# A Mamba and mixture-of-experts block on one core: the first state of batches 1 to 5 is multiplied by C's column in the banks

## The reference, cut to what matters

```python
delta = softplus(dt_raw @ dt_proj_w.T + dt_proj_b)          # 512 x 256 per batch
dA  = exp(einsum('bti,is->btis', delta, A))                 # 16 states s
dBu = einsum('bti,bts->btis', delta * u, B_ssm)
def step(h, inp):
    dA_t, dBu_t, C_t = inp
    h = dA_t * h + dBu_t
    return h, einsum('bis,bs->bi', h, C_t)
y = ys + u * D_param
y = y * silu(z)                                             # z gate
out = y @ out_proj_w.T + residual
# experts: h = silu(xf @ w_gate[e]) * (xf @ w_up[e]); out += gate * (h @ w_down[e])
```

## Time and profile before

| | |
|---|---|
| median of 3 runs | 611.23 us (609.09 to 611.37) |
| the profiled execution | 612.7 us, its span 610.9 us |
| PE, PEld | 541.7 us (89%), 422.0 us (69%) |
| DVE | 586.8 us (96%) |
| ACT, POOL | 459.0 us (75%), 490.1 us (80%) |
| mean granted clock of PE | 0.972 |

### The profile page before, as it was taken

The page is one execution under the profiler, slowest core; times in us unless marked ns, Lnnn a source line. Parts: engine busy times, 40 slices in busy tenths (PEclk is TensorE's granted clock), DMA queues, the critical chain, the costliest instruction groups (busy, mean ns, idle before and its releaser), DMA issues.

```text
span 610.9 us, 11399 instructions
## 1 busy us (share of the span) xinstructions
PE 541.7 (89%) x3558; PEld 422.0 (69%) x3558; DVE 586.8 (96%) x851; ACT 459.0 (75%) x927; POOL 490.1 (80%) x383
## 2 busy tenths in 40 slices
PE   5999889898898998999989999899989797768887
PEld 2377666656787778877887777877777565647564
DVE  6799989999999999999999999999999998998997
ACT  3699697259857888579876798667984589968880
POOL 2792466569999799988999889998997967875684
PEclk9899898979999999999999999999999899998999
DMA  7330219724796887879868898687874455323364
GB/s 194 111 130 1 74 32 251 280 81 160 253 314 217 282 283 236 305 236 310 294 171 309 283 291 298 209 288 248 282 261 155 155 222 193 104 99 104 80 134 90
DMA packets 61038, 122.48 MB, mean 200 GB/s; under 512 B 8362, under 2 KB 41778, under 8 KB 53938
## 3 DMA queue, kind: packets, MB, share of 16 engines
q1 hardware_dynamic: 53826, 112.42, 53.8%
q0 software_dynamic: 6144, 9.00, 7.1%
q10 hardware_dynamic: 1008, 0.33, 0.3%
HBM read 112.25 MB, written 9.47 MB: 199 GB/s over the span
## 4 chain that ended last, share of the span: by engine, by line
PE 53%; ACT 18%; DVE 15%; issue 12%; POOL 1%; ACTq 1%; DVEq 0%; POOLq 0%
PE bank L1483 9%; PE bank L1449 9%; PE bank L1601 8%; DVE bank L1161 6%; PE bank L1615 6%; PE bank L1609 5%; DVE h_sb L1178 5%; ACT dbu L556 3%; ACT bank L540 3%; ACT da L528 2%; PE bank L1506 2%; PE bank L1412 2%; PE bank L1498 2%; PE bank L1582 1%; PE bank L1357 1%
## 5 line engine op out<-in xcount | busy, mean ns | idle before, releaser
L948 POOL TENSOR_TENSOR dbu<-du,xn_all 128x1024 f32<-128x1024 f32 x86 | 203.7, 2369 | 24.4 <-DVE bank L1161 20.8
L1161 DVE TENSOR_TENSOR_SCAN bank<-bank,dbu 128x512 f32<-128x512 f32 x170 | 207.3, 1222 | 0.8
L1178 DVE TENSOR_TENSOR h_sb<-bank,xh_all 128x512 f32<-128x512 f32 x240 | 159.4, 678 | 1.2
L540 ACT ACTIVATE bank<-delta,a_sb 128x512 f32<-128x512 f32 x170 | 116.7, 688 | 38.2 <-DVE h_sb L1178 35.6
L1449 PE MATMUL bank<-id_sb,h_sb 128*128 128x128 f32 x992 | 132.7, 278 | 10.9 <-DVE h_sb L1178 9.4
L1449 PEld LDWEIGHTS bank<-id_sb,h_sb 128*128 128x128 f32 x992 | 113.5, 143 | 21.5 <-DVE h_sb L1178 14.7
L1161 DVE TENSOR_TENSOR_SCAN bank<-da,bank 128x512 f32<-128x512 f32 x82 | 96.3, 1213 | 6.2 <-PE bank L1412 5.1
L1601 PEld LDWEIGHTS bank<-wd_sb,hid 117*128 117x128 f32 (+1 forms) x432 | 54.7, 190 | 49.5 <-DVE hid L1212 29.3
L1601 PE MATMUL bank<-wd_sb,hid 117*128 117x128 f32 (+1 forms) x432 | 64.1, 284 | 18.7 <-ACT xT L721 16.5
L932 POOL DMA_INDIRECT xs<-xn_rows,src x72 | 70.4, 978 | 12.5 <-issue 9.0
L556 ACT ACTIVATE dbu<-du_t,bc_sb 128x256 f32<-128x256 f32 x164 | 69.4, 497 | 6.3 <-PE bank L1412 3.3
(11 more groups left out here) (200 smaller groups left out, 887.9 us busy)
## 6 DMA issues: line engine op xcount, KB each, us to landing
xh_all<-b_rows SPq DMA_DIRECT2D x30, 1024.0 KB
xn_all<-b_rows SPq DMA_DIRECT2D x25, 1024.0 KB
wgu_sb<-in_w_gu SPq DMA_DIRECT2D x72, 352.0 KB
wd_sb<-in_w_dn SPq DMA_DIRECT2D x72, 192.0 KB
y_slots<-ys SPq DMA_DIRECT2D x72, 64.0 KB
xn_rows<-xn_all SPq DMA_DIRECT2D x2, 1040.0 KB, 10.2
out<-x_sb SPq DMA_DIRECT2D x7, 256.0 KB
x_sb<-in_x SPq DMA_DIRECT2D x2, 640.0 KB, 6.0
```

The costliest lines, as they stand in the source:

```text
L540: nc.scalar.activation(bank_of(b, m)[:, :], delta[b % 2][:, hf, :], ACT.Exp, scale=a_sb[:, hf, k:k + 1]).then_inc(s["da_rdy"], 1)
L948: nc.gpsimd.tensor_tensor(dbu[k % 2][:, :, :], du[b % 2][:, :, :], b_ring[c % 2][:, k % CH, :].unsqueeze(1).to_broadcast([P, NH, T]), ALU. ...
L1161: nc.vector.tensor_tensor_scan(at, da_of(n)[:, hf, :] if n in IN_SBUF else at, inp, 0.0, ALU.mult, ALU.add).then_inc(s["h_rdy"], 1)
L1178: nc.vector.tensor_tensor(h_sb[k % 2][:, hf, :], bank_of(b, 2 * k + hf)[:, :], row, ALU.mult).then_inc(s["p_rdy"], 1)
```

## The change

In batches 1 to 5 (`BY_SCALAR`, steps 16, 32, 48, 64, 80) the scan of step 0 writes its state to `h_sb`, and there is no product for it. PE's `accumulate` of that step stands at the end of step 0, and not behind `up` in step 1. In step 1 ACT multiplies the four 128x256 pieces in banks 2 and 3 in place by C's column (`multiplied`); the sum of step 1 waits for that (`hc_rdy`). The column comes from `own_columns`: four PE transposes of 32 rows and a copy of 128x4 by ACT, for batch 1 in step 7 of batch 0, for batch 2 in step 5 of batch 1, for batches 3 to 5 in step 3 of the batch before. PE's `y_turn` stands ahead of `gate` in step 0. ACT's +1 of the z gate stands behind the next decay, `rounded` at the front of step 5 (end of step 4 before), `corrected` at the front of step 7 (end of step 5 before), the copy of `rows` and the multiplications ahead of `ys`. Waits on `p_rdy` count without the products that are gone (`by_vector`); where a bank's last reader was such a product the wait is for the scan (`bank_read`).

```diff
--- before.py
+++ after.py
@@ -197,7 +197,7 @@
                    first1 first2 first3 first4 first5 first6 first7 both0 both1 both2 both3 both4 both5 both6 both7 part_mm comb dbuT_a sp_corr a_ready stats_bn st rms_rt xn_w xh_w
                    xh_pe xhT_c lgmm oh_out rt top_rdy sel_rdy tot_mm tot_out rk_out slot_rdy texp_rdy lohi_rdy lo_rdy hi_set hi_rdy map_mm src_rdy
                    exp_rt x_pad acc_w g_mm u_mm bct_rdy dbu_p row_mm dbu_0 b_st b_in0 b_in1 c_in0 c_in1
-                   br_mm dbu_rdy da_rdy h_rdy p_rdy acc_mm y_out dd_rdy xc_mm x_th x_half u_rdy v_mm
+                   br_mm dbu_rdy da_rdy h_rdy p_rdy hc_rdy cc_mm cc_rdy acc_mm y_out dd_rdy xc_mm x_th x_half u_rdy v_mm
                    v_out bc_mm bc_rdy z_mm z_rdy z_one o_ev sp_exp sp_ln sp_rem sp_w sp_sum z_th delta_rdy du_rdy
                    dut_mm dut_rdy yb_mm g_rdy o_mm o_rdy o_out""".split()
         s = {k: sem(k) for k in names}
@@ -237,6 +237,19 @@
         def pooled_before(n):
 
             return sum(m < n for m in BY_POOL)
+
+        BY_SCALAR = [S * b for b in range(1, NB - 2)]
+
+        def by_vector(m):
+
+            return m - sum(min(max(m - 2 * n, 0), 2) for n in BY_SCALAR)
+
+        def bank_read(eng, m):
+
+            if m > 0 and (m - 1) // 2 in BY_SCALAR:
+                wait(eng, "h_rdy", m)
+            else:
+                wait(eng, "p_rdy", by_vector(m))
 
         def da_of(n):
 
@@ -257,6 +270,7 @@
         assert n0 == 2 * NT
 
         SKIPPED = {6: (1, 2), 7: (2, 4)}
+        COLUMN_TILE = {TILE[(b - 1) * S + (7 if b == 2 else 5)]: b for b in range(2, 6)}
         ROWS_AT = {b: 1 if b == 6 else 0 for b in range(NB - 1)}
         STEPS_AT = {b: (4, 6) if b == 6 else (2, 3) for b in range(NB - 1)}
         LOG_AT = {b: 10 if b == 6 else 9 for b in range(NB - 1)}
@@ -352,7 +366,7 @@
 
             def out_rows_in(b, c):
 
-                wait(sp, "p_rdy", 2 * S * b + 2 * CH * (c - 1) if b else 0)
+                wait(sp, "p_rdy", by_vector(2 * S * b + 2 * CH * (c - 1)) if b else 0)
                 spread_rows(c_ring[c % 2], b * 2 * S + S + c * CH, CH).then_inc(s[f"c_in{c % 2}"], 16)
 
             def own_rows(i):
@@ -532,7 +546,7 @@
 
                 b, k = n // S, n % S
                 m = 2 * k + hf
-                wait(act, "p_rdy", freed(b, m))
+                bank_read(act, freed(b, m))
                 if b == 6 and m == 2:
                     act.wait_ge(s["dut_rdy"], 3)
                 if k == 0:
@@ -592,6 +606,7 @@
                     vanishing(1, k - 7)
                 if k == 8:
                     totals_out()
+                    own_columns(1)
                 if k == 9:
                     spread_choices()
                     rounded(1)
@@ -630,6 +645,9 @@
                         scaled(g + 1)
                 if b < 6 and k == LOG_AT[b]:
                     logarithm(b + 1)
+                if g - 1 in BY_SCALAR:
+                    rows(b + 1)
+                    multiplied(g - 1)
                 if prev is not None and not (b < 6 and k == LOG_AT[b]):
                     out_out(prev)
                 if more:
@@ -640,6 +658,8 @@
                     scaled(g + 2)
                 if b < 6:
                     decay_bank(g + 1, 0)
+                    if k in z_step(b):
+                        z_plus(b, k)
                     if k == LOG_AT[b] and prev is not None:
                         out_out(prev)
                 elif b == 6 and k + 1 < S and g + 1 not in BY_PE:
@@ -660,8 +680,12 @@
 
             def early(b, k):
 
-                if k == ROWS_AT[b] + 1:
+                if b == 6 and k == ROWS_AT[b] + 1:
                     rows(b + 1)
+                if b < 6 and k == 5:
+                    rounded(b + 1)
+                if b < 6 and k == 7:
+                    corrected(b + 1)
                 if k in STEPS_AT[b]:
                     magnitudes(b + 1, STEPS_AT[b].index(k))
                 if b < 6 and k == PROJECT_AT[b] + 1:
@@ -675,9 +699,8 @@
 
                 if k in STEPS_AT[b]:
                     vanishing(b + 1, STEPS_AT[b].index(k))
-                if k == STEPS_AT[b][1] + 1:
+                if b == 6 and k == 7:
                     rounded(b + 1)
-                if k == (7 if b == 6 else 5):
                     corrected(b + 1)
                 if k == COLS_AT.get(b):
                     columns(b + 1)
@@ -696,15 +719,38 @@
                         act.wait_ge(s["dbuT_a"], S - 1)
                     nc.scalar.activation(du_t[:, hf, :], z_bank(b)[:, :], ACT.Copy)
                 nc.scalar.activation(zs_sb[:, hf, :], z_bank(b)[:, :], ACT.Tanh, scale=0.5).then_inc(s["z_th"], 1)
-                if 0 < b < 6:
-                    act.wait_ge(s["z_th"], 2 * b + i + 1)
-                    nc.scalar.activation(zs_sb[:, hf, :], zs_sb[:, hf, :], ACT.Identity, bias=sign_sb[:, 0:1]).then_inc(s["z_one"], 1)
+
+            def z_plus(b, k):
+
+                i, hf = z_turn(b, k), z_step(b)[k]
+                act.wait_ge(s["z_th"], 2 * b + i + 1)
+                nc.scalar.activation(zs_sb[:, hf, :], zs_sb[:, hf, :], ACT.Identity, bias=sign_sb[:, 0:1]).then_inc(s["z_one"], 1)
 
             def projected(b):
 
                 act.wait_ge(s["o_mm"], b + 1)
                 act.wait_ge(s["z_rdy"], 2 * b + 3)
                 nc.scalar.activation(du_t[:, 1, :], FB[0][:, :], ACT.Copy).then_inc(s["o_ev"], 1)
+
+            def multiplied(n):
+
+                b, k = n // S, n % S
+                i0 = BY_SCALAR.index(n)
+                if 0 < b < 6:
+                    act.wait_ge(s["cc_rdy"], b)
+                for i in range(2):
+                    act.wait_ge(s["acc_mm"], 2 * n + i + 1)
+                    for t in (2 * i, 2 * i + 1):
+                        last = nc.scalar.activation(HT[i][:, t % 2, :], HT[i][:, t % 2, :], ACT.Copy,
+                                                    scale=bc_sb[b % 2][:, t, S + k:S + k + 1])
+                    last.then_inc(s["hc_rdy"], 1)
+
+            def own_columns(c):
+
+                act.wait_ge(s["cc_mm"], c)
+                at = XHB if c == 1 else XD
+                nc.scalar.activation(bc_sb[c % 2][:, :, S:S + 1], at[:, 2 * P:3 * P].rearrange("p (t c) -> p t c", t=TT)[:, :, S:S + 1],
+                                     ACT.Copy).then_inc(s["cc_rdy"], 1)
 
             def y_evac(b):
 
@@ -717,6 +763,8 @@
             def slots_out(j):
 
                 act.wait_ge(s["xt_mm"], j + 1)
+                if j in COLUMN_TILE:
+                    own_columns(COLUMN_TILE[j])
                 wait(act, "u_mm", j - 1)
                 nc.scalar.activation(xT[j % 2][:, :], XD[:, 0:P], ACT.Copy).then_inc(s["xt_rdy"], 1)
                 if j == 0:
@@ -1008,7 +1056,7 @@
                     if i == 0:
                         pool.wait_ge(s["h_rdy"], 2 * (S * b + k) + 1)
                     else:
-                        pool.wait_ge(s["p_rdy"], 2 * (S * b + k) + i)
+                        pool.wait_ge(s["p_rdy"], by_vector(2 * (S * b + k) + i))
                     gathered(b0, c, t)
 
             scaled(S)
@@ -1157,19 +1205,25 @@
                 if b == NB - 1 and k == 1 and hf == 0:
                     dve.wait_ge(s["dut_rdy"], 6)
                 elif b == NB - 1 and k == 1:
-                    wait(dve, "p_rdy", 2 * S * b + 1)
-                nc.vector.tensor_tensor_scan(at, da_of(n)[:, hf, :] if n in IN_SBUF else at, inp, 0.0,
+                    bank_read(dve, 2 * S * b + 1)
+                to = at
+                if n in BY_SCALAR:
+                    to = h_sb[k % 2][:, hf, :]
+                    wait(dve, "acc_mm", 2 * (n - 1))
+                nc.vector.tensor_tensor_scan(to, da_of(n)[:, hf, :] if n in IN_SBUF else at, inp, 0.0,
                                              ALU.mult, ALU.add).then_inc(s["h_rdy"], 1)
 
             def product(b, k, hf):
 
                 c = k // CH
+                if b * S + k in BY_SCALAR:
+                    return
                 if b == 0 and c < 2:
                     if k % 2 == 0 and hf == 0:
                         dve.wait_ge(s[f"c_own{k // 2}"], 16)
                     row = own[k // 2][:, k % 2, :]
                 else:
-                    if k % CH == 0 and hf == 0:
+                    if hf == 0 and (k % CH == 0 or b * S + k - 1 in BY_SCALAR):
                         dve.wait_ge(s[f"c_in{c % 2}"], 16 * ((b - 1) * 2 + c // 2 + 2) if b else 16)
                     row = c_ring[c % 2][:, k % CH, :]
                 if hf == 0:
@@ -1394,6 +1448,8 @@
 
                 pe.wait_ge(s["lo_rdy"], g + 1)
                 pe.wait_ge(s["hi_rdy"], g + 1)
+                if g == 0:
+                    pe.wait_ge(s["cc_rdy"], 1)
                 at = g // (NT // NG8) * NJ
                 for i in range(NG8):
                     MM(MAP[:, at:at + NJ], lo_oh[g % NSLOT][:, :, i], hi_val[g % NSLOT][:, :, i], start=(g == 0 and i == 0),
@@ -1406,7 +1462,7 @@
                 n = b * S + k
```

(31 more changed lines are left out.)

## The result

The changed kernel takes **606.89 us** (median of 5 runs, 606.02 to 607.71), the kernel before 610.51 beside it (5 runs, 609.09 to 611.37): ratio **0.9948**, 95% interval 0.9932 to 0.9965. It is faster by 3.6 us between the medians, by the ratio 3.2 us (2.1 to 4.2). The profiled execution of after is 606.02 us, span 604.2.

What follows compares the result with a forecast made beforehand. From batch start to step 10 PE and ACT were taken to carry the chain, DVE keeping up with 0.1 us to spare. Terms 0.6 (batch 0) + 0.6 (batches 2 to 4) + 0 = +1.2 gave 612.4 us, range 607.5 to 614.5.

Steps and rivals of the forecast that it cites:

- The hand-off in step 1: DVE's second_product in step 1 waits for PE's up; of 1.18 us relief about 0.4 is left at step 2.
- The new waits: In step 1 of batches 2 to 5, DVE waits 0.6 to 0.9 us at second_product for PE's up.
- The multiplications: ACT's four new 128x256 multiplications in step 1 take 1.6 us, hidden with 0.1 to 0.3 us of cover.
- `own_columns` in batch 3: At step 3 the column's transposes take 0.44 us on PE and cost +0.2 ahead of the next xT.
- the moved pieces ... so 0: Rounding and correction move to steps 5 and 7, where PE sets the pace and ACT has gaps: cost 0.
- Step 10: Sign in the profile after: DVE waits over 0.4 us at the scan of step 10.
- Batches 2 to 4: The column's transposes at step 3 delay ACT's part of the chain: +0.2 us per batch, +0.6 in all.
- Batch 0: The column's transposes stand on the chain between skip term and step matmuls: +0.6 us (0.3 to 0.9).
- The end of batch 0 and batch 1: Batch 1 was taken at 0 (-0.5 to +0.4); the sum had no term for DVE's relief at batch 0's end.
- DVE alone is the bound: Rival: all 5.9 us of DVE's relief come back, less batch 0's 0.6, giving 605.9 us; chance 0.15.
- The tie at step 10 loosens: Rival: transposes hidden, 0.4 per batch of 2 to 5 and 0.5 of batch 1 kept: 609.7 us; chance 0.2.
- The slower one: Rival: ACT in step 1 becomes the bound, each multiplication in the bank taking 0.69 us: 616.7 us; chance 0.1.

Runs made afterwards that it cites:

- rounding_back: The changed kernel with rounding and correction put back at the ends of steps 4 and 5; 607.68 us, ratio 0.9969 to the kernel before.
- products_gone: The kernel before without DVE's ten products or any replacement, and with y_turn ahead of gate; 607.67 us, ratio 0.9964.
- no_columns: The changed kernel without own_columns, its multiplications taking another column already there; 607.36 us, ratio 0.9957 to the kernel before.
- gone_and_rounding: The kernel before without the ten products, y_turn ahead of gate, and rounding and correction at the fronts of steps 5 and 7; 606.70 us, ratio 0.9953.
- dve_back: The changed kernel plus two dummy DVE products per batch, both inputs in SBUF, in batches 1 to 5; 626.23 us, ratio 1.0273 to the kernel before.
- dve_back_bank: The changed kernel plus two dummy DVE products per batch, one input in a bank, in batches 2 to 5; 609.31 us, ratio 0.9988.

## Why the prediction was wrong

The picture of the bound held in the main: for batches 2 to 4 the relief of DVE alone is worth 0.05 us, because a row over PE and ACT is as long to step 10 as DVE's. What failed was one term at nil (the moved rounding), DVE's relief taken at nil at the end of batch 0 and in batch 1, and two prices for the column that weren't paid. On the ruler: -0.94, -1.3, and 0.6 twice, with -0.13 in b5; together they are the 3.6 us between +1.2 and -2.4.

**A misreading.** I read the gap of 0.1 at step 10 as room that DVE had to spare, with PE and ACT last. The rows before it say otherwise. DVE in before, batch 3:

```profile
305.93 0.68 DVE L1178 TENSOR_TENSOR h_sb<-bank,xh_all 128x512 f32<-128x512 f32 x1
```

This product ends at 306.61, and ACT's decay ahead of the logarithm, which needs its bank, starts at 306.64. From that decay to the one of step 10 are 4.37 us, in every kernel here, so the gap of 0.12 is what remains when DVE itself comes last. ACT would have been ready only 0.05 us earlier (from the start of its instruction before to this one are 0.33 us, and 0.28 where it doesn't wait). In after the same decay starts 0.10 behind the product and ACT comes last, by 0.06. So in batch 3 of before DVE was last by 0.05, which fits that the relief alone gave 0.05 and the moved rounding alone nothing.

**Right.** *The hand-off in step 1*: 0.4 ahead at step 2, found 8.73 - 8.34 = 0.39. *The new waits*: right in sum and not in place. I said 0.6 to 0.9 at `second_product` in step 1; it is 0.35 there and 0.29 earlier, at `gate(b-1)`, which waits for PE's `y_turn` and which I had at no cost: 0.64 together. *The multiplications*: 1.6 us, found 1.54, hidden: the next xT starts 9.32 us after the batch's first `accumulate` (271.99 - 262.67), before 9.37. (What I set against them, the section on the TRN2 errata in the Trainium skill's VectorE: DVE Perf Modes, is about operations whose source is SBUF; these read a bank.) *`own_columns` in batch 3*: 0.44 us on PE, found 0.43, and +0.2 in front of the next xT. That xT starts 18.05 us after the batch's first `accumulate` (280.72 - 262.67), against 17.79 before (283.99 - 266.20): +0.26.

**The step that failed: "the moved pieces ... so 0".** I wrote that between 288.95 and 303.5 PE sets the pace and ACT has gaps. PE in before does run there without a gap that the view marks, but twice it starts `down` just behind what it needs: in step 7 behind ACT's xT, in step 6 behind DVE's `second_product`. ACT, DVE and PE in before, batch 3, steps 5 to 8:

```profile
292.90 1.15 ACT L790 ACTIVATE sp_e<-sp_d,sign_sb 128x1024 f32<-128x1024 f32 x1
...
297.53 0.26 ACT L721 ACTIVATE xT<-bank 128x128 f32<-128x128 f32 x1
```

```profile
292.38 0.54 DVE L1212 TENSOR_TENSOR hid<-ga,bank 118x384 f32<-118x384 f32 x1
```

```profile
296.08 1.88 PE L1483 MATMUL bank<-xhT,wk_sb 128*128 128x512 f32 x4
297.94 0.91 PE L1601 MATMUL bank<-wd_sb,hid 117*128 117x128 f32 x6
...
302.69 0.83 PE L1601 MATMUL bank<-wd_sb,hid 117*128 117x128 f32 x6
```

The `conv` matmuls to the next `down` are 1.86 us apart here, and 1.71 where PE doesn't wait for xT (297.19 to 298.90 in after): 0.15 of waiting, too short to be marked. xT ends at 297.79, `down` starts at 297.94. Such crumbs add up. In step 6 `second_product` ends at 292.92 and `down` starts at 292.98. In before PE needs 302.69 - 288.95 = 13.74 us from the `down` of step 5 to that of step 8 (the earlier trace rows has the first), in after 298.90 - 285.53 = 13.37:

```profile
285.53 0.91 PE L1672 MATMUL bank<-wd_sb,hid 117*128 117x128 f32 x6 [1.09 <-ACT xT L769]
...
297.19 1.88 PE L1541 MATMUL bank<-xhT,wk_sb 128*128 128x512 f32 x4
298.90 0.83 PE L1672 MATMUL bank<-wd_sb,hid 117*128 117x128 f32 x6
```

The cause of the larger part stands in ACT's row. In before one interval between two xT, 292.46 to 297.53, holds the correction (1.15 us) and the three operations of the z gate, 5.07 us in all. In after they are in two intervals, of 4.39 and 4.22 us (xT at 289.05, 293.44 and 297.66). From the `down` of step 5 to that of step 6 are 4.03 us in before and 3.93 in after and in rounding_back, where DVE is ahead: that 0.10 goes with DVE's relief. From step 6 to step 8 are 9.71 in before, 9.67 in rounding_back and 9.44 in after: 0.23 of it is the moved rounding. The 0.37 pays for the 0.11 by which PE's `down` at step 5 came later (22.86 against 22.75 after the first `accumulate`), and the scan of step 10 starts 0.32 earlier, 45.22 instead of 45.54 (311.74 - 266.20). The period is shorter by 0.31. rounding_back gives 0.24 of that back, which is the size of the term that I had at 0. The other 0.07 is about the size of what DVE's relief gives alone, 0.05 in products_gone.

**Step 10.** I said a wait of over 0.4; it is 0.17, for the same reason: the chain it waits for had come forward. With the chain left as it was, rounding_back shows 0.41 and products_gone 0.58.

**Batches 2 to 4: +0.6 forecast, -0.94 found.** The +0.26 in front of xT in batch 3 was right there, but `down` at step 5 came only 0.11 later, and 0.05 per batch is left (no_columns). The moved rounding, which pays only together with DVE's relief, wasn't in the sum.

**Batch 0: +0.6 forecast, 0.07 found** from the skip matmuls to the ranking (11.51 against 11.44). I priced the new matmuls as if they stood alone in PE's row; they ran among the step matmuls, and the two together took no longer than the step matmuls alone in before (1.08 and 1.13 us).

**The end of batch 0 and batch 1: 0 forecast, -0.6 and -0.7 found.** These carry more than half of the ruler's gain, and this is the second step that failed: "taken: 0" for batch 1, and nothing in the sum for the end of batch 0. Ahead of the first gate DVE was dense before; in after the two scans stand back to back:

```profile
118.92 2.33 DVE L1213 TENSOR_TENSOR_SCAN h_sb<-bank,dbu 128x512 f32<-128x512 f32 x2
122.14 1.28 DVE L1240 TENSOR_TENSOR g_sb<-zs_sb,bank 128x512 f32<-128x512 f32 x2 [0.89 <-PE bank L1603]
```

From the first of them to the gate are 3.22 us; before, scan, product, scan and product took 3.82 (121.66 to 125.48). I had looked at step 2 of batch 1 alone and not at what stands before the gate; nor had I asked whether the row of PE and ACT is independent of DVE where it begins without expert tiles. In batch 1 it isn't: in products_gone ACT's decay ahead of the logarithm starts 0.04 us behind DVE's product there, so it moved forward with DVE, and in batches 2 to 5 0.50 behind. DVE's relief counts, and products_gone alone has 0.9 in b1. Here the rival "DVE alone is the bound" (605.9) was right, for the end of batch 0 and for batch 1.

**The rivals.** "The tie at step 10 loosens" had the right sign and place, and its 609.7 too little. The slower one fell at 0.39 us per multiplication. The mistake in the chances was to treat "which row is the bound" as one question for all batches.

**What stays open.** Whether there is any gain outside the ruler: its -2.4 and the ratio's -3.2 (-2.1 to -4.2) agree within the noise, and the first steps of batch 0 scatter by 2 us. What the moved `y_turn` is worth by itself, and ACT's other moves (the z gate's +1, the copy of `rows` ahead of `ys`), was not tested.

**What bounds it now.** The chain of after in order of time, batch 3 into batch 4 (start, us, what), shows a third row that is tied with the two:

```profile
262.67 1.09 PE bank L1507 x8
...
278.71 1.15 DVE bank L1213
279.86 0.07 issue
279.93 2.36 POOL dbu L996
```

```profile
332.28 2.33 POOL dbu L996
334.61 0.04 DVEq L209
334.64 0.29 DVE h_sb L1232
334.93 0.04 issue
334.98 1.09 PE bank L1507 x8
```

POOL is dense from step 4 to the end of the batch. Its last `dbu` ahead of the new batch is done at 334.61, and DVE's next scan starts at 334.84. So POOL is about 0.2 us from setting the pace, and DVE and ACT at step 10 are within 0.06 us of each other. The chain's 34% for POOL probably comes from that: with a tie the view follows one of two rows, and a change of 0.1 us turns its shares over. In gone_and_rounding, 0.1 us per batch faster, POOL's share is 4%.

## What to carry to other kernels

Where two rows end at the same point, test an edit on each alone and then both: here they gave 0.05, nothing, and 0.43 us per batch. A small gap ahead of an engine isn't slack when what it waits for was itself started by that engine's work a few us before: follow the wait back one more instruction. Compare kernels timed on different occasions by their ratio to the same kernel before. An engine without marked gaps may still be paced by another; compare the distance of the same two instructions at a place where the operand was early; and before a term is set at nil because "the engine has gaps", see whether the piece stands ahead of something that the tied row reads. Ask which row is the bound stage by stage, and take a second profile of the kernel before, which shows what part of a difference is scatter.

## What the runs showed of the hardware

A DVE `tensor_tensor` of 128x512 f32 with both inputs in SBUF took 1.55, 2.33 and 2.60 us when it was started during POOL's 128x1024 `tensor_tensor`, each ending 0.55 to 0.56 us behind POOL's end, and 0.69 where it was started before POOL's (dve_back); with a bank as one input it took 0.67 (dve_back_bank): a dummy that is to stand for real work must have its operands in the same memories. Four multiplications of 128x256 by ACT from a bank into the same bank cost 1.54 us, 0.39 each, no more than the four from SBUF to SBUF in the earlier trace rows (1.71), and the scan into SBUF was no slower than the one into a bank: 1213 ns a piece over ten, beside 1222 ns over 160. The groups of after:

```profile
L1213 DVE TENSOR_TENSOR_SCAN h_sb<-bank,dbu 128x512 f32<-128x512 f32 x10 | 12.0, 1213 | 0.0
L1213 DVE TENSOR_TENSOR_SCAN bank<-bank,dbu 128x512 f32<-128x512 f32 x160 | 195.2, 1222 | 1.0 <-ACT bank L554 0.7
```
